# Second cross-attention: integer queries in 48 rows, with the scale applied during the search for the maximum

## The chip, the cores and the metric

The kernel runs on one core of one Trainium2 chip. The metric is the device time of one execution in microseconds (us). Three timed runs of the kernel before gave 736.27, 737.52 and 738.99 us, so the median is 737.52 us. One more execution was taken with the hardware profiler: its own time is 730.36 us, and all rows below come from it.

## The reference, cut to what matters

The program is two layers of a perceiver: cross-attention, a sequence mixer and a mixture of experts in each. The change touches the cross-attention of layer 1 alone. It has 256 query rows (x) and 4096 context rows, 16 heads of 16 channels:

```python
q = (x @ Wq + bq);  k, v = split(cond @ Wkv + bkv)      # 16 heads x 16 channels
q = _fq_sym(q * scale, axis=-1)    # s = max|q| / 127 over the 16 channels; round(q / s) * s
k = _fq_sym(k, axis=-1)            # the same for every key and head
v = _fq_sym(v, axis=2)
attn = softmax(einsum('bhqd,bhkd->bhqk', q, k))
attn = _fq_unsigned(attn, axis=-1) # round(attn / (max / 255)) * (max / 255)
out = einsum('bhqk,bhkd->bhqd', attn, v) @ Wp + bp
```

So each quantized query is an integer between -127 and 127 times one scale for each (query, head).

## The kernel before, in words

Two stages matter. Their queues are written out by hand: every engine has its own program, and semaphores order them. No scheduler moves anything.

**kv_stage** (names k_...) first makes the queries. TensorE multiplies the normed x with Wq (L1563), VectorE adds the bias (L1425), and quantize_queries (L1296 to L1321) quantizes them. The scores must be as exact as an f32 product, while TensorE is to run on bf16. So the quantized query (integer times scale, L1306) is split into three bf16 parts, and the quantized key likewise. Six products of parts are kept (PRODUCTS), which makes 6 x 16 = 96 rows of contraction for one head. The six columns of each query element are written by six casts: three copies of part 0 (L1315), a subtraction (L1318), two copies of part 1 (L1315), a subtraction (L1320), one copy of part 2 (L1321). All of this stands in VectorE's queue before the first step on the keys.

Then 16 steps of 256 keys each follow. In step m TensorE projects keys and values of step m+2 (L1575, L1577), VectorE quantizes the keys (L1446 to L1453), ScalarE and GpSimd split them into three bf16 parts (L1535, L1491, L1543, L1493), TensorE transposes the parts (L1592), and they are stored to kT_scratch in HBM (L1530). TensorE projects steps 0 and 1 in advance; the projection of step 2 waits until VectorE has read the keys of step 0 out of PSUM (semaphore k_read, from L1449). The transposes of step m wait for part 2 of the keys from GpSimd (L1493).

**xattn1_stage** (names d_...) handles the 16 heads one after the other. For one head there are 8 tiles ("quarters") j = 0..7: two halves of the queries (t) times four quarters (f) of 1024 keys. For each quarter:

- TensorE makes the scores, two matmuls of 512 columns (L1949), into one of three PSUM slots of 1024 columns (quarter). It waits for the ScalarE read that frees the slot.
- VectorE finds the negated maximum of each row over the 1024 columns (search, L1795). After four quarters L1799 combines four of them.
- ScalarE takes exp(score - maximum) with the sum (L1887).
- GpSimd scales and rounds the result to f16 (L1773). Half of the quarters are turned by DMA (L1736), the other half by TensorE (L1976), with copies out of PSUM by VectorE (L1807) and ScalarE (L1899). TensorE multiplies with the values (L1992) one head later. Once in a head VectorE rounds the values of that head (L1820).

The keys of a head come from kT_scratch in 6 DMAs of 16 rows (one for each product, L1723), issued on the SP queue. For heads 0 and 1 all 12 stand at the beginning; those of head m+2 stand behind the DMA transposes of head m. The stages run behind one another, with a barrier between them.

Of the kernel before, what the change touches and what calls it, by code (L numbers as in the profile page):

```python
# [22 lines left out]
NEG = 1e30  # L23
# [20 lines left out]
H, HD = 16, 16  # L44
# [1233 lines left out]
def layer1_memory(nc, d, g, sb, sem):  # L1278
    g["v"] = sb("v", [P, NKC, D])
    g["vam"] = sb("v_absmax", [P, D])  # L1280
    g["qs"] = sb("qs", [P, TC, H, 100], BF16)
    g["kT_stored"] = [sem(f"kT_stored{s}") for s in range(2)]
    g["w_inT"] = sb("w_inT", [P, KC, 2 * INNER])
    g["w_inT_in"] = sem("w_inT_in")
# [5 lines left out]
    g["w1_in"] = sem("w1_in")  # L1290


PRODUCTS = ((0, 0), (0, 1), (0, 2), (1, 0), (1, 1), (2, 0))
QROWS = len(PRODUCTS) * HD


def quantize_queries(nc, step, src, scaled, out, rest, s, rs, absmax, qs, done):

    f3, i3, q3, r3 = (a[:, :, :].rearrange("p t (h e) -> p (t h) e", e=HD) for a in (src, scaled, out, rest))
    axes = [P, TC * H, HD]  # L1300
    step(nc.vector.tensor_reduce(absmax, f3, AX.X, ALU.max, apply_absolute_value=True))
    step(nc.vector.tensor_scalar(s, absmax, 1.0 / 127.0, 1e-8, ALU.mult, ALU.max))
    step(nc.vector.reciprocal(rs, s))
    step(nc.vector.tensor_tensor(i3, f3, rs.unsqueeze(2).to_broadcast(axes), ALU.mult))
    step(nc.vector.tensor_scalar(i3, i3, ROUND, ROUND, ALU.add, ALU.subtract))
    step(nc.vector.tensor_tensor(q3, i3, s.unsqueeze(2).to_broadcast(axes), ALU.mult))  # L1306

    def columns(part):

        by_row = qs[:, :, :, 0:QROWS].rearrange("p t h (e j) -> p (t h) e j", j=len(PRODUCTS))  # L1310
        return [by_row[:, :, :, j] for j, (pq, _) in enumerate(PRODUCTS) if pq == part]

    def part_to(src_, part):
        for c in columns(part):
            step(nc.vector.tensor_copy(c, src_))  # L1315
        return columns(part)[0]
    p0 = part_to(q3, 0)
    step(nc.vector.tensor_tensor(r3, q3, p0, ALU.subtract))  # L1318
    p1 = part_to(r3, 1)
    step(nc.vector.tensor_tensor(q3, r3, p1, ALU.subtract))  # L1320
    nc.vector.tensor_copy(columns(2)[0], q3).then_inc(done, 1)  # L1321


def kv_stage(nc, d, g):
    ctx, sb, banks, sem = scope(nc)
# [3 lines left out]
    with ctx:  # L1329
# [10 lines left out]
        rest = [sb(f"k_rest{s}", [P, KPS, D]) for s in range(2)]  # L1340
        parts = [sb(f"k_parts{s}", [P, K_PARTS, KPS, D], BF16) for s in range(2)]
        kT = [sb(f"k_kT{s}", [P, K_PARTS * KC, KEYS], BF16) for s in range(2)]
        am = sb("k_absmax", [P, KPS * H])
        sc = sb("k_scale", [P, KPS * H])
# [52 lines left out]
        with nc.Block() as block:  # L1397
# [18 lines left out]
            def _(dve):  # L1416
# [7 lines left out]
                dve.wait_ge(q_psum, 1)  # L1424
                step(nc.vector.scalar_tensor_tensor(qf[:, :, :], ps[:, 5, :].rearrange("p (t c) -> p t c", t=TC), HD ** -0.5,  # L1425
                                                    bq[:, :].unsqueeze(1).to_broadcast([P, TC, D]), ALU.mult, ALU.add))
                quantize_queries(nc, step, qf, qi, qq, qr, sc[:, :], rs[:, :], am[:, :], g["qs"], qs_ready)
                lead = step.n

                def copy_turned(m, s, i):  # L1430
# [174 lines left out]
def xattn1_stage(nc, d, g):  # L1605
# [14 lines left out]
    with ctx:  # L1620
# [4 lines left out]
        qs = g["qs"]  # L1625
# [86 lines left out]
        with nc.Block() as block:  # L1712
# [66 lines left out]
            def _(dve):  # L1779
# [12 lines left out]
                def search(m, j):  # L1792
                    t, f = j // QT, j % QT
                    dve.wait_ge(scores_ready, m * APH + (j + 1))
                    nc.vector.tensor_reduce(nm[:, t, m:m + 1, f:f + 1], quarter(m, j).unsqueeze(1), AX.X, ALU.max,  # L1795
                                            negate=True).then_inc(nm_ready, 1)
                    if f == QT - 1:
                        dve.wait_ge(nm_ready, m * APH + (j + 1))
                        nc.vector.tensor_scalar(raised[:, :], nm[:, t, m, :], LOG255, NEG, ALU.add, ALU.min,  # L1799
                                                accum_out=mb[:, t, m, QT - 1:QT]).then_inc(mb_ready, 1)  # L1800
# [73 lines left out]
            def _(act):  # L1874
# [7 lines left out]
                def exps(m, j):  # L1882
                    t, f = j // QT, j % QT
                    act.wait_ge(nm_ready, m * APH + (j + 1))
                    if 1 <= m < H:
                        act.wait_ge(r_ready, m * APH + (j + 1 - APH))
                    nc.scalar.activation(e[j].unsqueeze(1), quarter(m, j).unsqueeze(1), ACT.Exp, bias=nm[:, t, m:m + 1, f],  # L1887
                                         accum_out=zp[:, t, m:m + 1, f]).then_inc(e_ready, 1)
                    if f == QT - 1:
                        act.wait_ge(mb_ready, m * TC + (t + 1))  # L1890
                        nc.scalar.activation(lift[t][:, :].unsqueeze(1), nm[:, t, m:m + 1, :], ACT.Exp, scale=-1.0,  # L1891
                                             bias=mb[:, t, m:m + 1, QT - 1]).then_inc(lift_ready, 1)
# [419 lines left out]
```

## Time and profile before

| | us |
|---|---|
| median of three timed runs | 737.52 |
| the profiled execution, its own time | 730.36 |
| its span | 728.7 |
| VectorE busy in the span | 494.4 (68%) |
| TensorE busy in the span | 624.3 (86%) |
| ScalarE busy in the span | 381.4 (52%) |
| GpSimd busy in the span | 334.5 (46%) |

The span is what the rows of the profile cover; the execution's own time is 1.7 us longer. The timed runs are about 7 us longer than the profiled one, so sums are made against the profiled one. The shares of busy time are averages over stages that have little in common: kv_stage runs from about 290 to 391 us, xattn1_stage from about 391 to 603 us, and each must be read by itself. A row of a list of instructions gives the start, the duration and, in brackets, how long the engine had been idle and what ended that. On VectorE an instruction may start while the last tens of nanoseconds of the one before it still show; the distance from start to start is what the queue pays.

### The profile page before, as it was taken

The page shows a single profiled execution, that of the slowest core. Times are in us where ns is not written, and L with a number is a line of the kernel's source. Part 1 is how long each engine was busy: PE and PEld are TensorE (multiplying, and loading weights), DVE is VectorE, ACT ScalarE, POOL GpSimd, SP SyncE. Part 2 cuts the span into 40 slices and gives each one's busy share as a digit, 9 for nine tenths or more (in the row PEclk, how much of TensorE's full clock was granted, in tenths as well). Part 3 has the DMA queues.
Part 4 walks back from the last instruction along what each step waited for, and adds up shares of the span by engine and source line. Part 5 has one row for each costly group of instructions (what it writes and reads, how often), then busy time and mean ns, then how long its engine had stood idle before and what let it go on. Part 6 is the DMA issues. An engine that isn't in the chain of part 4 may idle for free. (4 is left out here: it accounts for less than half of the span.)

```text
span 728.7 us, 13062 instructions
## 1 busy us (share of the span) xinstructions
PE 624.3 (86%) x4727; PEld 408.2 (56%) x4727; DVE 494.4 (68%) x813; ACT 381.4 (52%) x738; POOL 334.5 (46%) x261
## 2 busy tenths in 40 slices
PE   3767999986799999779995789888888889889997
PEld 1333445543577776558883155545554565667775
DVE  3268999974443333599994999999999955523222
ACT  1247865523211111336663899999999953222221
POOL 1039999981111110136651598898888940000000
PEclk9989999998699999979997596887879979999999
DMA  8827200004066660314444688788796938800000
GB/s 351 304 85 303 116 0 1 0 0 136 1 195 195 196 196 3 107 52 144 144 130 130 179 139 189 133 173 151 154 168 139 161 59 346 352 1 1 0 0 14
DMA packets 97030, 93.80 MB, mean 129 GB/s; under 512 B 70288, under 2 KB 87888, under 8 KB 92624
## 3 DMA queue, kind: packets, MB, share of 16 engines
q1 hardware_dynamic: 84432, 86.78, 43.5%
q10 hardware_dynamic: 12544, 6.29, 3.0%
q8 instruction: 34, 0.56, 0.3%
q14 instruction: 20, 0.16, 0.1%
HBM read 69.66 MB, written 6.62 MB: 105 GB/s over the span
## 5 line engine op out<-in xcount | busy, mean ns | idle before, releaser
L1795 DVE TENSOR_REDUCE d_nmax<-d_psum 128x1 f32<-128x1024 f32 x128 | 151.8, 1213 | 7.8 <-PE d_psum L1949 7.5
L1949 PE MATMUL d_psum<-d_kst,d_qT 96*128 96x512 bf16 x256 | 94.9, 465 | 27.6 <-DMA d_kst<-kT_scratch 10.6
L425 POOL TENSOR_TENSOR b_h<-b_h,b_cb 128x1024 f32<-128x1024 f32 x32 | 87.8, 2743 | 6.7 <-DVE b_h L475 5.1
L1887 ACT ACTIVATE d_e<-d_psum,d_nmax 128x1024 f32<-128x1024 f32 x64 | 71.4, 1120 | 14.8 <-DVE d_nmax L1795 14.1
L1773 POOL TENSOR_SCALAR d_rounded<-w_early,d_lift 128x1024 f16<-128x1024 f32 x62 | 70.1, 1131 | 14.0 <-ACT d_lift L1891 9.5
L1773 POOL TENSOR_SCALAR d_rounded<-d_e,d_lift 128x1024 f16<-128x1024 f32 x64 | 72.9, 1139 | 7.0 <-ACT d_lift L1891 1.3
L475 DVE TENSOR_TENSOR_SCAN b_h<-b_dA,b_psum 128x1024 f32<-128x1024 f32 x32 | 73.1, 2285 | 2.5 <-ACT b_dA L530 2.0
L1575 PE MATMUL k_psum<-k_wkv,k_ctxT 128*128 128x256 f32 x256 | 67.1, 394 | 6.2 <-issue 6.2
L1887 ACT ACTIVATE w_early<-d_psum,d_nmax 128x1024 f32<-128x1024 f32 x64 | 71.4, 1121 | 0.1
L530 ACT ACTIVATE b_dA<-b_dtT,b_A 128x248 f32<-128x248 f32 x128 | 53.7, 490 | 33.1 <-DVE b_h L475 28.1
L586 PE MATMUL b_psum<-b_bdiag,b_dtx 128*128 128x512 f32 x128 | 60.2, 594 | 0.8 <-DVE b_h L475 0.8
L1976 PEld LDWEIGHTS d_psum<-d_ident_f,d_rounded 128*128 128x128 f16 x512 | 41.8, 116 | 32.7 <-issue 21.7
L1575 PEld LDWEIGHTS k_psum<-k_wkv,k_ctxT 128*128 128x128 f32 x256 | 45.5, 198 | 16.9 <-issue 7.4
L1976 PE MATMUL d_psum<-d_ident_f,d_rounded 128*128 128x128 f16 x512 | 48.9, 252 | 6.8 <-ACT d_probsT L1899 3.6
L1949 PEld LDWEIGHTS d_psum<-d_kst,d_qT 96*128 96x128 bf16 x256 | 18.9, 108 | 57.7 <-ACT d_e L1887 26.4
L837 POOL TENSOR_TENSOR c_pick_weighed<-c_pick,c_w 128x384 f32<-128x384 bf16 x16 | 13.3, 833 | 81.2 <-PE c_psum L1033 74.3
L1992 PEld LDWEIGHTS d_psum<-d_vh,d_probsT 128*128 128x128 f16 x1024 | 42.9, 97 | 8.8 <-issue 4.0
L1992 PE MATMUL d_psum<-d_vh,d_probsT 128*128 128x16 f16 x1024 | 43.5, 170 | 2.3 <-issue 1.6
L607 PE MATMUL b_psum<-b_h,ident 128*128 128x256 f32 x128 | 36.1, 404 | 6.9 <-DVE b_h L482 4.4
L872 DVE TENSOR_TENSOR c_a<-c_silu,c_psum 128x192 f32<-128x192 f32 x16 | 5.7, 354 | 52.9 <-ACT c_silu L932 52.9
L607 PEld LDWEIGHTS b_psum<-b_h,ident 128*128 128x128 f32 x128 | 21.8, 189 | 33.9 <-DVE b_h L482 32.2
L1232 PE MATMUL f_psum<-w,f_xnT 128*128 (+1 forms) x128 | 40.5, 459 | 0.0
(396 smaller groups left out, 1194.1 us busy)
## 6 DMA issues: line engine op xcount, KB each, us to landing
d_kst<-kT_scratch SPq DMA_DIRECT2D x96, 128.0 KB, 2.8
w<-in_w SPq DMA_DIRECT2D x8, 1088.0 KB, 20.3
b_cb<-c_scratch SPq DMA_DIRECT2D x4, 2048.0 KB, 6.8
w_early<-in_w0gu SPq DMA_DIRECT2D x8, 768.0 KB, 5.2
w_late<-in_w0gu SPq DMA_DIRECT2D x8, 768.0 KB, 5.1
kT_scratch<-k_kT ACTq DMA_DIRECT2D x16, 384.0 KB, 2.8
a_ctxT<-in_ctxT SPq DMA_DIRECT2D x2, 2048.0 KB, 12.2
a_ctx<-in_ctx SPq DMA_DIRECT2D x2, 2048.0 KB, 20.6
```

Source lines behind the costliest of these rows:

```text
L425: nc.gpsimd.tensor_tensor(hv, hv, cv, ALU.mult).then_inc(hc_ready, 1)
L475: nc.vector.tensor_tensor_scan(h[s][:, :], dA[s % 2][:, :], ps[:, 2 * (s % 2):2 * (s % 2) + 2, :] .rearrange("p a b -> p (a b)"), 0.0, ALU ...
L530: nc.scalar.activation(out[:, :, j, :, 1:L], src, ACT.Exp, scale=A[:, c, n * NT + j:n * NT + j + 1]).then_inc(dA_ready, 1)
L586: last = nc.tensor.matmul(ps[:, 2 * (s % 2) + t, :], dtx[:, t, c * P:(c + 1) * P], bdiag[t][:, n * NT:n * NT + NT, :], start=True, stop=True)
L607: last = nc.tensor.matmul(ps[:, 4 + c, 0:T], ident[:, :], hv[:, j], start=False, stop=False, skip_group_check=True)
L1575: nc.tensor.matmul(psum_kv(s, part)[:, j, :], cT[s][:, k, j * P:(j + 1) * P], wkv[:, k, cols], start=(k == 0), stop=False)
L1773: nc.gpsimd.tensor_scalar(tile_of(r, j), e[j], lift[t][:, f:f + 1], HALF_ULP_ONE, ALU.mult, ALU.add).then_inc(r_ready, 1)
L1795: nc.vector.tensor_reduce(nm[:, t, m:m + 1, f:f + 1], quarter(m, j).unsqueeze(1), AX.X, ALU.max, negate=True).then_inc(nm_ready, 1)
L1887: nc.scalar.activation(e[j].unsqueeze(1), quarter(m, j).unsqueeze(1), ACT.Exp, bias=nm[:, t, m:m + 1, f], accum_out=zp[:, t, m:m + 1, f]). ...
L1949: last = nc.tensor.matmul(quarter(m, j)[:, b * 512:(b + 1) * 512], qT[0:QROWS, m:m + 1, t * P:(t + 1) * P], kst[m % 2][0:QROWS, at:at + 51 ...
L1976: last = nc.tensor.transpose(turn_tile(m, j)[:, b * P:(b + 1) * P], tile_of(r, j)[:, b * P:(b + 1) * P], ident16[:, :])
L1992: last = nc.tensor.matmul(out, pT[m % 2][:, t, b, :], vh[m % 2][:, b, :], start=(b == 0), stop=(b == NKC - 1 and t not in BY_DMA))
```

## The change

The query is kept as its integer, which is exact in one bf16 part, so only three products are left (integer with each of the three key parts), and a head has 48 rows in place of 96. The scale is not in the product any more. The negated scale of each query and head goes into a new tile, minus_sq. The search does three things in one instruction: it multiplies the 1024 scores in PSUM by the negated scale, writes them back to the same place, and takes the minimum of the results (accum_out). ScalarE's exp reads the negated scores with scale=-1.0.

```diff
-PRODUCTS = ((0, 0), (0, 1), (0, 2), (1, 0), (1, 1), (2, 0))
+PRODUCTS = ((0, 0), (0, 1), (0, 2))
...
-    g["qs"] = sb("qs", [P, TC, H, 100], BF16)
+    g["qs"] = sb("qs", [P, TC, H, 52], BF16)
+    g["minus_sq"] = sb("minus_q_scale", [P, TC, H])
...
     step(nc.vector.tensor_scalar(i3, i3, ROUND, ROUND, ALU.add, ALU.subtract))
-    step(nc.vector.tensor_tensor(q3, i3, s.unsqueeze(2).to_broadcast(axes), ALU.mult))
...
-    p0 = part_to(q3, 0)
-    step(nc.vector.tensor_tensor(r3, q3, p0, ALU.subtract))
-    p1 = part_to(r3, 1)
-    step(nc.vector.tensor_tensor(q3, r3, p1, ALU.subtract))
-    nc.vector.tensor_copy(columns(2)[0], q3).then_inc(done, 1)
+    step(nc.vector.tensor_scalar(minus_s.rearrange("p t h -> p (t h)"), s, -1.0, None, ALU.mult))
+    by_row = qs[:, :, :, 0:QROWS].rearrange("p t h (e j) -> p (t h) e j", j=len(PRODUCTS))
+    nc.vector.tensor_copy(by_row, i3.unsqueeze(3).to_broadcast(axes + [len(PRODUCTS)])).then_inc(done, 1)
...
                 def search(m, j):
-                    nc.vector.tensor_reduce(nm[:, t, m:m + 1, f:f + 1], quarter(m, j).unsqueeze(1), AX.X, ALU.max,
-                                            negate=True).then_inc(nm_ready, 1)
+                    nc.vector.tensor_scalar(quarter(m, j), quarter(m, j), g["minus_sq"][:, t, m:m + 1], NEG, ALU.mult, ALU.min,
+                                            accum_out=nm[:, t, m, f:f + 1]).then_inc(nm_ready, 1)
...
-                    nc.scalar.activation(e[j].unsqueeze(1), quarter(m, j).unsqueeze(1), ACT.Exp, bias=nm[:, t, m:m + 1, f],
+                    nc.scalar.activation(e[j].unsqueeze(1), quarter(m, j).unsqueeze(1), ACT.Exp, scale=-1.0, bias=nm[:, t, m:m + 1, f],
```

The lines of the changed kernel are numbered 14 lower from kv_stage on, and in quantize_queries they are shifted as well. Its order of instructions stands beside that of before at three places. VectorE's queue in kv_stage, from the rounding of the query (k_qi) to the first step on the keys; before:

```order
L1305 TENSOR_SCALAR k_qi<-k_qi 128x512
L1306 TENSOR_TENSOR k_qq<-k_qi,k_scale 128x512
L1315 CAST qs<-k_qq 128x32x16 x3
L1318 TENSOR_TENSOR k_qrest<-k_qq,qs 128x512
L1315 CAST qs<-k_qrest 128x32x16 x2
L1320 TENSOR_TENSOR k_qq<-k_qrest,qs 128x512
L1321 CAST qs<-k_qq 128x32x16
L1446 TENSOR_REDUCE k_absmax<-k_psum 128x32
```

and now:

```order
L1306 TENSOR_SCALAR k_qi<-k_qi 128x512
L1307 TENSOR_SCALAR minus_q_scale<-k_scale 128x32
L1309 CAST qs<-k_qi 128x32x48
L1432 TENSOR_REDUCE k_absmax<-k_psum 128x32
L1433 TENSOR_SCALAR k_scale<-k_absmax 128x32
```

Nine instructions of 512 elements are gone; one of 32 elements and one of 1536 elements stand in their place. VectorE's queue in xattn1_stage, one head from the rounding of its values (d_vh) on; before:

```order
L1820 TENSOR_SCALAR d_vh<-d_vh_scaled 128x512
L1795 TENSOR_REDUCE d_nmax<-d_psum 128x1 x3
L1812 COPY d_o<-d_psum 128x2x16
L1795 TENSOR_REDUCE d_nmax<-d_psum 128x1
L1799 TENSOR_SCALAR d_nmax_raised,d_mm_log<-d_nmax 128x4
L1795 TENSOR_REDUCE d_nmax<-d_psum 128x1
L1807 TENSOR_SCALAR d_probsT<-d_psum 128x1024
```

and now:

```order
L1806 TENSOR_SCALAR d_vh<-d_vh_scaled 128x512
L1781 TENSOR_SCALAR d_psum,d_nmax<-d_psum,minus_q_scale 128x1024 x3
L1798 COPY d_o<-d_psum 128x2x16
L1781 TENSOR_SCALAR d_psum,d_nmax<-d_psum,minus_q_scale 128x1024
L1785 TENSOR_SCALAR d_nmax_raised,d_mm_log<-d_nmax 128x4
L1781 TENSOR_SCALAR d_psum,d_nmax<-d_psum,minus_q_scale 128x1024
L1793 TENSOR_SCALAR d_probsT<-d_psum 128x1024
```

Nothing moves there; each search is another kind of instruction with two outputs and one more input. The SP queue from the start of xattn1_stage, with the loads of the keys (d_kst); before:

```order
L1723 DMA d_kst<-kT_scratch 16x4096 x12
L1728 DMA d_wp<-in_wp 128x512
L1728 DMA d_bp<-in_bp 128x256
L1729 DMA w_inT<-in_w_inT 128x2048
L1736 DMA_TRANSPOSE d_probsT<-d_rounded 128x16x128 x2
L1723 DMA d_kst<-kT_scratch 16x4096 x6
```

and now:

```order
L1709 DMA d_kst<-kT_scratch 16x4096 x6
L1714 DMA d_wp<-in_wp 128x512
L1714 DMA d_bp<-in_bp 128x256
L1715 DMA w_inT<-in_w_inT 128x2048
L1722 DMA_TRANSPOSE d_probsT<-d_rounded 128x16x128 x2
L1709 DMA d_kst<-kT_scratch 16x4096 x3
```

Half of the loads are gone, and the rest keep their place behind the transposes.

## Rows read from the trace of the kernel before

**Rows 1.** Busy time by engine in four stretches: three of kv_stage, one of xattn1_stage.

```profile
core 0: us, PE busy (x) PEld busy (x) DVE busy (x) ACT busy (x) POOL busy (x), PEclk, DMA share, GB/s
308.20:314.40 6.20, 0.03 (x1) 0.00 (x0) 5.93 (x10) 0.00 (x0) 0.00 (x0) 0.68 0.15 42
314.40:320.00 5.60, 5.57 (x14) 4.04 (x15) 5.36 (x10) 1.75 (x3) 2.49 (x2) 0.50 0.00 0
...
325.00:382.00 57.00, 57.00 (x394) 46.86 (x393) 53.55 (x98) 38.95 (x49) 34.51 (x26) 1.00 0.48 139
...
412.20:586.90 174.70, 149.02 (x2110) 93.29 (x2110) 170.86 (x242) 168.68 (x300) 154.15 (x136) 0.84 0.83 155
```

**Rows 2.** Who waited for whom from 412.2 to 586.9 us: total, times, longest.

```profile
PE d_psum L1949 <- DMA d_kst<-kT_scratch: 5.8, 7, 1.2
...
DVE d_nmax L1795 <- PE d_psum L1949: 2.4, 9, 0.4
```

**Rows 3.** VectorE in order of time, one head: start us, us, instruction.

```profile
481.87 0.43 DVE L1820 TENSOR_SCALAR d_vh<-d_vh_scaled 128x512 f16<-128x512 f32 x1
482.22 3.48 DVE L1795 TENSOR_REDUCE d_nmax<-d_psum 128x1 f32<-128x1024 f32 x3
...
486.96 0.16 DVE L1799 TENSOR_SCALAR_CACHE_REDUCE d_nmax_raised<-d_nmax 128x4 f32<-128x4 f32 x1
487.04 0.08 DVE L1799 DVE_READ_ACCUMULATOR d_nmax_raised<-d_nmax 128x1 f32 x1
487.04 1.22 DVE L1795 TENSOR_REDUCE d_nmax<-d_psum 128x1 f32<-128x1024 f32 x1
...
492.96 0.85 DVE L1820 TENSOR_SCALAR d_vh<-d_vh_scaled 128x512 f16<-128x512 f32 x1
```

**Rows 4.** VectorE's groups by form: busy us, mean ns of one, idle before.

```profile
L1795 DVE TENSOR_REDUCE d_nmax<-d_psum 128x1 f32<-128x1024 f32 x128 | 151.8, 1213 | 7.8 <-PE d_psum L1949 7.5
L475 DVE TENSOR_TENSOR_SCAN b_h<-b_dA,b_psum 128x1024 f32<-128x1024 f32 x32 | 73.1, 2285 | 2.5 <-ACT b_dA L530 2.0 <-PE b_psum L586 0.4
...
L1446 DVE TENSOR_REDUCE k_absmax<-k_psum 128x32 f32<-128x512 f32 x16 | 11.0, 688 | 1.1
...
L454 DVE TENSOR_SCALAR b_h<-b_psum,b_cols 128x256 f32<-128x256 f32 x2 | 1.0, 485 | 0.1
...
L448 DVE TENSOR_SCALAR b_psum<-b_psum 128x512 f32<-128x512 f32 x1 | 0.7, 700 | 1.1 <-ACT b_psum L509 1.1
...
L443 DVE COPY b_drT<-b_psum 128x256 f32<-128x256 f32 x1 | 0.4, 425 | 2.1 <-PE b_psum L552 2.1
```

**Rows 5.** VectorE in order of time, the query's quantization.

```profile
301.98 0.18 DVE L1302 TENSOR_SCALAR k_scale<-k_absmax 128x32 f32<-128x32 f32 x1
...
303.77 0.69 DVE L1306 TENSOR_TENSOR k_qq<-k_qi,k_scale 128x512 f32<-128x512 f32 x1
304.50 3.18 DVE L1315 CAST qs<-k_qq 128x512 bf16<-128x512 f32 x3
...
312.36 0.64 DVE L1446 TENSOR_REDUCE k_absmax<-k_psum 128x32 f32<-128x512 f32 x1
```

**Rows 6.** TensorE, then GpSimd, in order of time, the first steps on the keys.

```profile
314.44 2.04 PE L1575 MATMUL k_psum<-k_wkv,k_ctxT 128*128 128x256 f32 x4 [6.20 <-issue]
...
320.33 1.19 PE L1575 MATMUL k_psum<-k_wkv,k_ctxT 128*128 128x256 f32 x4
...
323.17 1.03 PE L1575 MATMUL k_psum<-k_wkv,k_ctxT 128*128 128x256 f32 x4
...
324.15 1.03 PE L1575 MATMUL k_psum<-k_wkv,k_ctxT 128*128 128x256 f32 x4
```

```profile
318.34 1.16 POOL L1493 TENSOR_TENSOR k_parts<-k_rest,k_parts 128x512 bf16<-128x512 f32 x1 [0.74 <-ACT k_parts L1543]
```

**Rows 7.** All engines in order of time, the start of xattn1_stage.

```profile
393.75 7.55 SPq L1723 DMA_DIRECT2D d_kst<-kT_scratch  x12
...
399.59 2.72 PE L1949 MATMUL d_psum<-d_kst,d_qT 96*128 96x512 bf16 x6 [4.80 <-DMA d_kst<-kT_scratch]
```

More of the change, by code:

```diff
@@ L1290, in layer1_experts, with quantize_queries @@
     g["w1_in"] = sem("w1_in")
-PRODUCTS = ((0, 0), (0, 1), (0, 2), (1, 0), (1, 1), (2, 0))
+PRODUCTS = ((0, 0), (0, 1), (0, 2))
 QROWS = len(PRODUCTS) * HD
-def quantize_queries(nc, step, src, scaled, out, rest, s, rs, absmax, qs, done):
-    f3, i3, q3, r3 = (a[:, :, :].rearrange("p t (h e) -> p (t h) e", e=HD) for a in (src, scaled, out, rest))
+def quantize_queries(nc, step, src, scaled, s, rs, absmax, qs, minus_s, done):
+    f3, i3 = (a[:, :, :].rearrange("p t (h e) -> p (t h) e", e=HD) for a in (src, scaled))
     axes = [P, TC * H, HD]
@@ L1305, in quantize_queries @@
     step(nc.vector.tensor_scalar(i3, i3, ROUND, ROUND, ALU.add, ALU.subtract))
-    step(nc.vector.tensor_tensor(q3, i3, s.unsqueeze(2).to_broadcast(axes), ALU.mult))
[L1308 to L1316, printed above, removed]
-    p0 = part_to(q3, 0)
-    step(nc.vector.tensor_tensor(r3, q3, p0, ALU.subtract))
-    p1 = part_to(r3, 1)
-    step(nc.vector.tensor_tensor(q3, r3, p1, ALU.subtract))
-    nc.vector.tensor_copy(columns(2)[0], q3).then_inc(done, 1)
+    step(nc.vector.tensor_scalar(minus_s.rearrange("p t h -> p (t h)"), s, -1.0, None, ALU.mult))
+    by_row = qs[:, :, :, 0:QROWS].rearrange("p t h (e j) -> p (t h) e j", j=len(PRODUCTS))
+    nc.vector.tensor_copy(by_row, i3.unsqueeze(3).to_broadcast(axes + [len(PRODUCTS)])).then_inc(done, 1)
 def kv_stage(nc, d, g):
@@ L1351, in kv_stage @@
         qi = sb("k_qi", [P, TC, D])
-        qq = sb("k_qq", [P, TC, D])
-        qr = sb("k_qrest", [P, TC, D])
         ps = banks("k_psum")
@@ L1426, in _ @@
                                                     bq[:, :].unsqueeze(1).to_broadcast([P, TC, D]), ALU.mult, ALU.add))
-                quantize_queries(nc, step, qf, qi, qq, qr, sc[:, :], rs[:, :], am[:, :], g["qs"], qs_ready)
+                quantize_queries(nc, step, qf, qi, sc[:, :], rs[:, :], am[:, :], g["qs"], g["minus_sq"][:, :, :], qs_ready)
                 lead = step.n
```

## The prediction

> **What bounds the kernel now.** I read the busy time by stretches first, then the waits inside the two stages that the change touches, then VectorE in order of time, and last the groups by form, for prices.
>
> From 412.2 to 586.9 us, which is 15 heads of the second cross-attention, VectorE is busy 170.86 of 174.70 us and ScalarE 168.68 [rows 1]. VectorE waits there only 2.4 us in nine short waits, all for scores [rows 2]. So its queue sets the pace: 174.7 / 15 = 11.65 us for one head. The shortest head is 11.09 us, from 481.87 to 492.96 [rows 3]. Three searches take 3.48 us in a row there, with the last one shown at its full 1.21, so searches start 1.13 us apart: 1.21 less an overlap of 0.08. Eight of them are 9.1 us of the 11.09. The mean head is 0.56 longer: 0.16 is the waits (2.4 / 15), and much of the rest is the rounding of the values, which took 0.43 us in one head and 0.85 in the next [rows 3].
>
> In kv_stage TensorE is busy 57.00 of 57.00 us once the steps on the keys run [rows 1]: it sets the pace there. But before that it stands idle for 6.20 us, from 308.2 to 314.44, until VectorE has got through the queries and has read the keys of step 0. The granted clock is then at its lower level (0.50, or 1.2 GHz) from 314.4 to 320 [rows 1, 6].
>
> **Part 1: the query's quantization.** From L1306 to the first L1446 VectorE spends 312.36 - 303.77 = 8.59 us [rows 5]. All of it goes. What comes instead is a negation of 32 elements, 0.18 us as the same form L1302 and 0.04 to the next start, and one copy that writes 1536 elements. No row shows that form. Below, one strided cast of today, 3.18 / 3 = 1.06 us [rows 5], if its 512 reads are what costs. Above, three of them, 3.18 us, if each written element costs. Its destination is contiguous, not stepped as today's, so I take one element a clock: 1.13 us for 1024 [rows 3] makes 1.7 for 1536. VectorE reaches the keys 8.59 - 0.22 - 1.7 = 6.7 us earlier (5.2 to 7.3).
>
> TensorE then starts the projection of step 2 at once, at 308.2, and saves 6.2 us of idle time. It also never drops its clock: three groups took 320.33 - 314.44 = 5.89 us at the lower clock, against 0.98 each later (324.15 - 323.17) [rows 6], so 2.95 more. Something new is late next. The transposes of step 0 stand in TensorE's queue behind that projection and need part 2 from GpSimd, which ended at 318.34 + 1.16 = 319.50 [rows 6] and now ends 6.7 earlier, at 312.8, while the projection ends at 308.2 + 3.9 = 312.1. That is a wait of 0.7 us; I allow the step after it the same again, and a little more, 1.6 in all. While TensorE waits, the projection and the transposes behind it wait too. Gain: 6.2 + 2.95 - 1.6 = 7.5 us (6.0 to 8.5). As TensorE bounds the rest of the stage, nothing there gives it back.
>
> **Part 2: the loads of the keys.** Twelve DMAs take 7.55 us to issue, 0.63 each, and TensorE waits for head 0's six, until 399.59 [rows 7]. With three in place of six it starts 3 x 0.63 = 1.9 us earlier (1.0 to 2.0). Later heads have three DMAs less each. TensorE waited 5.8 us for those keys in seven heads [rows 2], but it is up to three quarters ahead, and little of that reached VectorE: of its 2.4 us of waits I credit 1.6 to earlier keys and to a VectorE that asks later. Half as many rows leave the length of a matmul alone (it streams 512 columns either way), so TensorE's work on scores costs the same: 0.
>
> **Part 3: the search, 128 times.** Three things are new in it.
> - Its kind and its write to PSUM. A reduction over 512 elements of PSUM takes 688 ns, a tensor_scalar from PSUM back to the same PSUM 700 ns [rows 4]: 0 to +12 ns. It works at one element a clock both ways. I take 3.
> - The scale, one value for each partition. With one such operand 256 elements from PSUM take 485 ns, a copy without one 425 [rows 4]: +60 ns. [...]
> - The minimum, read out by a second instruction. In L1799 that reading shows 83 ns, but it starts 0.08 after the main part and the next search starts in the same hundredth: 487.04 and 487.04 [rows 3]. The price in the queue is 0, and it ends with the main part. That is behind 4 elements; behind 1024 it could be the whole 0.08. I take 0, because it is the only row of this pair.
>
> So 128 x 0.064 = +8.2 us on VectorE's queue (0 to 18.4). Nothing else queued there is shorter, so it all stands on the path, apart from the 1.6 us above: +6.6. ScalarE works 168.68 / 15 = 11.2 us a head, below VectorE's new 11.09 + 0.51 = 11.6. exp with a constant scale is the instruction of before: 0.
>
> The reading of the accumulator is where the Trainium skill disagrees. The page "VectorE: DVE Perf Modes", section "Two Vector instructions with no wait between them", says that an operation with an accumulator output is two instructions, and "Vector Engine (DVE) Microarchitecture Reference", section 5.2, gives about 75 ns of fixed cost to each instruction after overlap. By that the readings would add 128 x 0.075 = 9.6 us. The trace agrees on two instructions, but not on their price: 0.00 from start to start [rows 3]. The same section names no price for a scalar operand, and by it alone the search would be as long as now; the row of L454 against L443 says 60 ns.
>
> **The sum.** -7.5 - 1.9 + 6.6 = -2.8 us. Against the profiled execution's 730.36 us that is 727.6. The timed runs were 7.2 us above it; the same difference on their median gives 737.52 - 2.8 = 734.7 us. Its own range, from the bounds of parts 1 and 2 and a rounding of the values that may fall into step with GpSimd by some 0.2 us a head either way (3 us): 731 to 738.5.
>
> **Rivals.**
> 1. The reading costs its 0.08 us behind a long stream. Place: between any two searches, 128 times. 128 x 0.08 = +10.2, net +7.4: 745. It decides against the change as soon as a reading costs more than 0.02 us (2.8 / 128). For it: the instruction is 83 ns long; against it: 32 pairs in which the next one doesn't wait.
> 2. The search doesn't get longer: scale and reading vanish in the overlap, or the new kind has a shorter fixed part. Part 3 is then 0, and of the 1.6 us of waits only what earlier keys take away stays, a quarter of it, 0.4: -7.5 - 1.9 - 0.4 = -9.8, 727.7. Against it is L454.
> 3. Multiplying and accumulating together take two clocks an element, as the scan does: 2285 ns for 1024 [rows 4]. 128 x 1.07 = +137, about 865. For it: also a chain of multiply and combine; against it: the reduction keeps one a clock with an accumulator of its own.
> 4. Part 1 isn't passed on: TensorE, freed early, waits for the split of the keys on ScalarE and GpSimd in every step. 7.5 becomes 0: +4.7, 742.2. For it: TensorE and GpSimd are nearly level (57.00 against the chain that it waits for); against it: GpSimd is busy only 34.51 of 57.00 [rows 1].
>
> **How the numbers follow.** A measurement of this kernel can tell about 0.5%, 3.7 us, from no change. My forecast gets 0.51, rival 1 0.19, rival 2 0.17, rival 3 0.06, rival 4 0.05, and 0.02 is for what I haven't seen. Faster by over 0.5% (below 733.8): rival 2 and four tenths of the forecast, 0.37. Slower by over 0.5% (above 741.2): rivals 1, 3 and most of 4, 0.31. The rest, 0.32, is within. The range takes in the forecast, rival 1 and nearly all of rival 2, and leaves out rival 3: 727 to 746. The likeliest case alone is 731 to 738.5.
>
> **What would show it.** In the changed profile: the search as a main part of about 1.27 us and a reading of 0.08, with searches in a row 1.19 us apart (1.27 for rival 1, 1.13 for rival 2, over 2.2 for rival 3); a head of about 11.6 us at the shortest; the copy of the query at about 1.7 us; no idle time of TensorE over 1.5 us between its projections of steps 1 and 2, and a granted clock of 1.00 there; the stage of the keys 7 to 8 us shorter; the first scores about 4 us after SP starts to issue keys, not 5.8. The prediction is wrong if VectorE isn't busy over 95% of the heads any more, if searches are further apart than 1.22 us, or if TensorE waits in every step on the keys.

## The result and the profile after

The changed kernel takes 766.88 us (median of 4 runs, 765.86 to 770.47), the kernel before 738.25 in runs beside it: a ratio of 1.040 (1.035 to 1.044), so 28.6 us slower. Forecast were 734.7 and a range of 727 to 746. The profiled execution of after took 765.86 us, with a span of 764.0, against 728.7 before: 35.3 us more. The execution profiled before was itself 7.9 us under the median given here, so the two traces lie further apart than the medians. The kernel before took 727 to 747 us over the sessions, so each experiment is judged by its ratio to runs of that kernel taken beside it, fast runs against fast ones; by the means of all runs, x1 and x5 below would both be 1.007 in place of 1.009 and 1.014, and no other ratio moves by over 0.003.

By stage, from the two traces: the work ahead of the queries (not changed) takes 2.1 us less. The stage of the keys, from k_qf (the bias added to the queries) to the first load of keys, takes 93.5 us, 93.2 before. From that load to the first scores it is 6.0, 5.8 before, and from the first scores to the end of the attention 238.7, 201.7 before. So all of the loss is in the heads, and nothing was gained ahead of them.

**The heads.** Busy time by engine of after in four stretches of heads, to be held against the last row of [rows 1]:

```profile
core 0: us, PE busy (x) PEld busy (x) DVE busy (x) ACT busy (x) POOL busy (x), PEclk, DMA share, GB/s
...
440.00:480.00 40.00, 40.00 (x400) 20.22 (x396) 34.53 (x67) 32.84 (x57) 30.32 (x27) 0.50 0.61 101
480.00:520.00 40.00, 40.00 (x422) 20.48 (x420) 34.50 (x70) 33.15 (x57) 28.61 (x26) 0.50 0.55 103
520.00:560.00 40.00, 40.00 (x421) 20.27 (x420) 34.58 (x70) 32.79 (x58) 28.41 (x26) 0.50 0.64 110
560.00:600.00 40.00, 40.00 (x420) 20.16 (x418) 34.51 (x67) 33.53 (x57) 29.13 (x27) 0.50 0.56 110
```

TensorE is busy without a gap in these stretches, and its granted clock is 0.50 (1.2 GHz) throughout; before it was 0.84 on average, with TensorE busy 149.0 of 174.7 us [rows 1]. VectorE, which set the pace before at 98%, is at 86%. Every head but the first takes 14.13 us, against a mean of 11.64 before: 15 heads are 14.03 on average, so 15 x 2.39 = 35.8 of the stage's 37.0 us.

The groups by form over the 15 heads of after, and what VectorE waits for in the same stretch (us in total, times, longest):

```profile
L1781 DVE TENSOR_SCALAR_CACHE_REDUCE d_psum<-d_psum,minus_q_scale 128x1024 f32<-128x1024 f32 x120 | 153.4, 1290 | 25.3 <-PE d_psum L1935 22.8
L1935 PE MATMUL d_psum<-d_kst,d_qT 48*128 48x512 bf16 x238 | 117.8, 621 | 1.3 <-ACT d_e L1873 1.0 <-ACT w_early L1873 0.3
```

```profile
DVE d_psum L1781 <- PE d_psum L1935: 22.8, 29, 1.1
```

So VectorE now waits 22.8 us for scores, against 2.4 before [rows 2]. The score matmul, the same 512 columns, takes 621 ns; before, from the same kind of view:

```profile
L1949 PE MATMUL d_psum<-d_kst,d_qT 96*128 96x512 bf16 x238 | 86.0, 453 | 19.2 <-ACT d_e L1887 6.8 <-DMA d_kst<-kT_scratch 5.8 <-ACT w_early L1887 5.5
```

The search itself, VectorE of after in order of time, against [rows 3]:

```profile
480.67 1.29 DVE L1781 TENSOR_SCALAR_CACHE_REDUCE d_psum<-d_psum,minus_q_scale 128x1024 f32<-128x1024 f32 x1
481.88 0.14 DVE L1781 DVE_READ_ACCUMULATOR d_psum<-d_psum,minus_q_scale 128x1 f32 x1
481.88 1.29 DVE L1781 TENSOR_SCALAR_CACHE_REDUCE d_psum<-d_psum,minus_q_scale 128x1024 f32<-128x1024 f32 x1
```

1.29 us long, 1.21 from start to start; 1.13 before. The reading starts with the next search in the same hundredth.

**The stage of the keys.** VectorE of after in order of time, the end of the query's work (against [rows 5]):

```profile
301.20 0.43 DVE L1306 TENSOR_SCALAR k_qi<-k_qi 128x512 f32<-128x512 f32 x1
301.66 0.18 DVE L1307 TENSOR_SCALAR minus_q_scale<-k_scale 128x32 f32<-128x32 f32 x1
301.88 0.96 DVE L1309 CAST qs<-k_qi 128x1536 bf16<-128x1536 f32 x1
302.76 0.68 DVE L1432 TENSOR_REDUCE k_absmax<-k_psum 128x32 f32<-128x512 f32 x1
```

The 8.59 us are 302.76 - 301.66 = 1.10 now: VectorE comes 7.5 us earlier. TensorE doesn't stand idle at the start any more, and its clock stays at 1.00:

```profile
302.00:307.90 5.90, 5.90 (x32) 4.70 (x31) 5.66 (x11) 1.71 (x3) 1.20 (x1) 1.00 0.20 56
```

Yet the stage isn't shorter, because each step got longer. GpSimd and VectorE around one instruction, k_ki, before and then after:

```profile
337.72 0.43 DVE L1451 TENSOR_SCALAR k_ki<-k_ki 128x512 f32<-128x512 f32 x1
...
338.39 1.51 POOL L1493 TENSOR_TENSOR k_parts<-k_rest,k_parts 128x512 bf16<-128x512 f32 x1 [1.85 <-ACT k_parts L1543]
...
342.37 0.43 DVE L1451 TENSOR_SCALAR k_ki<-k_ki 128x512 f32<-128x512 f32 x1
```

```profile
340.27 1.15 POOL L1479 TENSOR_TENSOR k_parts<-k_rest,k_parts 128x512 bf16<-128x512 f32 x1 [1.00 <-ACT k_parts L1529]
...
340.45 1.25 DVE L1437 TENSOR_SCALAR k_ki<-k_ki 128x512 f32<-128x512 f32 x1
...
341.48 0.84 PE L1578 MATMUL k_psum<-ident_bf,k_parts 128*128 128x128 bf16 x12 [0.34 <-POOL k_parts L1479]
...
345.69 1.26 DVE L1437 TENSOR_SCALAR k_ki<-k_ki 128x512 f32<-128x512 f32 x1
```

Before, k_ki starts 0.7 us ahead of GpSimd's second subtraction and takes 0.43; steps are 4.65 us apart. After, it starts 0.18 behind that subtraction, ends 0.28 behind its end and takes 1.25; steps are 5.25 apart, and TensorE waits for GpSimd in each of them (0.3 to 0.4 us, and 1.8 at the end of the loop). The Trainium skill ("SBUF — State Buffer", section "Who interferes with whom") has the rule: VectorE and GpSimd share a port pair under an exclusive lock, tensor_scalar can need both ports, and whoever starts first holds the pair to the end. The trace agrees: once the steps are 5.25 us apart, k_ki ends just behind GpSimd's instruction and never inside it. Before, GpSimd's second subtraction was the longer one, 1.44 to 1.61 us against 1.15 now, and the steps were shorter all the same.

**The first scores.** TensorE's wait there, of after (against [rows 7]):

```profile
396.35 1.15 POOL L1736 PARTITION_ALL_REDUCE d_v_absmax<-v_absmax  x1 [12.95 <-issue]
...
397.38 0.28 POOL L1737 MEMSET d_minus<- 128x128 f16 x1
...
397.92 2.71 PE L1935 MATMUL d_psum<-d_kst,d_qT 48*128 48x512 bf16 x6 [4.21 <-POOL d_minus L1737]
```

The keys need three loads instead of six, but TensorE waits for a GpSimd memset that stands behind an all-reduce.

### The profile page after: what moved, and what is told of

Its sections match the earlier page's. It is cut to its first block and busy times, and to the rows that moved or that the text cites. A ratio compares the mean times of both kernels' runs of the same rounds, so it can differ in the third digit from the quotient of the medians.

```text
span 764.0 us, 13135 instructions
## 1 busy us (share of the span) xinstructions
PE 683.8 (89%) x4727; PEld 418.4 (55%) x4727; DVE 509.8 (67%) x934; ACT 385.6 (50%) x738; POOL 328.8 (43%) x261
## 5 line engine op out<-in xcount | busy, mean ns | idle before, releaser
L1781 DVE TENSOR_SCALAR_CACHE_REDUCE d_psum<-d_psum,minus_q_scale 128x1024 f32<-128x1024 f32 x128 | 163.3, 1289 | 29.9 <-PE d_psum L1935 27.3
L1935 PE MATMUL d_psum<-d_kst,d_qT 48*128 48x512 bf16 x256 | 126.7, 621 | 9.7 <-ACT d_e L1873 4.4
L1873 ACT ACTIVATE d_e<-d_psum,d_nmax 128x1024 f32<-128x1024 f32 x64 | 71.3, 1114 | 36.6 <-DVE d_psum L1781 35.8
L1962 PEld LDWEIGHTS d_psum<-d_ident_f,d_rounded 128*128 128x128 f16 x512 | 49.5, 142 | 52.9 <-POOL d_rounded L1759 39.0
L1962 PE MATMUL d_psum<-d_ident_f,d_rounded 128*128 128x128 f16 x512 | 66.1, 311 | 2.1 <-POOL d_rounded L1759 1.8
L1561 PE MATMUL k_psum<-k_wkv,k_ctxT 128*128 128x256 f32 x256 | 64.0, 381 | 0.0
L1561 PEld LDWEIGHTS k_psum<-k_wkv,k_ctxT 128*128 128x128 f32 x256 | 43.7, 190 | 9.9
L1935 PEld LDWEIGHTS d_psum<-d_kst,d_qT 48*128 48x128 bf16 x256 | 21.4, 116 | 47.8 <-issue 33.9
L1978 PE MATMUL d_psum<-d_vh,d_probsT 128*128 128x16 f16 x1024 | 45.8, 175 | 0.0
```

Source lines behind the costliest of these rows:

```text
L1561: nc.tensor.matmul(psum_kv(s, part)[:, j, :], cT[s][:, k, j * P:(j + 1) * P], wkv[:, k, cols], start=(k == 0), stop=False)
L1781: nc.vector.tensor_scalar(quarter(m, j), quarter(m, j), g["minus_sq"][:, t, m:m + 1], NEG, ALU.mult, ALU.min, accum_out=nm[:, t, m, f:f + ...
L1935: last = nc.tensor.matmul(quarter(m, j)[:, b * 512:(b + 1) * 512], qT[0:QROWS, m:m + 1, t * P:(t + 1) * P], kst[m % 2][0:QROWS, at:at + 51 ...
L1962: last = nc.tensor.transpose(turn_tile(m, j)[:, b * P:(b + 1) * P], tile_of(r, j)[:, b * P:(b + 1) * P], ident16[:, :])
L1978: last = nc.tensor.matmul(out, pT[m % 2][:, t, b, :], vh[m % 2][:, b, :], start=(b == 0), stop=(b == NKC - 1 and t not in BY_DMA))
```

## The experiments

Theory for the heads: the number of rows of the score matmul (its contraction) decides which clock is granted. 48 rows hold it at 0.50, TensorE becomes the bound, and the search costs what was forecast. Rivals: the new search, the number of loads, or the values in the rows do it. Theory for the keys: the steps are long because of the order in which GpSimd and VectorE meet, and a single delay decides it.

### Rows of the score matmul

**x1: the change with each product twice (96 rows).**

```diff
-PRODUCTS = ((0, 0), (0, 1), (0, 2))
+PRODUCTS = ((0, 0), (0, 1), (0, 2)) * 2
...
-    step(nc.vector.tensor_scalar(minus_s.rearrange("p t h -> p (t h)"), s, -1.0, None, ALU.mult))
+    step(nc.vector.tensor_scalar(minus_s.rearrange("p t h -> p (t h)"), s, -0.5, None, ALU.mult))
```

> The changed kernel with 96 rows again: the three products stand twice and the scale is halved, so the search, the queries and the result are those of the change, and only the contraction's rows (48 to 96) and the key loads (3 to 6 a head) go back. Theory (the rows decide the granted clock): the clock in the heads returns to about 0.84 as before, TensorE leaves the bound, and a head takes 12.1 us (11.65 of before and 0.06 for each of 8 searches) in place of 14.13: about 32 us less than the changed kernel, 733 to 745. Rival (the slower search holds the clock down, or its writes to PSUM do): the clock stays 0.50 and the time 765 or more.

739.26 us, ratio 1.0089 (1.0045 to 1.0132); heads 12.27 us on average, the granted clock of a head 0.59 to 1.00. Doubling the rows takes back three quarters of the loss. It brings back the six loads a head as well; x5 below keeps three.

**x2: the kernel before with 48 rows and its plain search** (only the first part of the query is kept; less is computed).

```diff
-PRODUCTS = ((0, 0), (0, 1), (0, 2), (1, 0), (1, 1), (2, 0))
+PRODUCTS = ((0, 0), (0, 1), (0, 2))
-    p0 = part_to(q3, 0)
...
+    for c in columns(0)[:-1]:
+        step(nc.vector.tensor_copy(c, q3))
+    nc.vector.tensor_copy(columns(0)[-1], q3).then_inc(done, 1)
```

> The kernel before with 48 rows alone: the queries keep only their first bf16 part, which leaves out the parts that carry the rest of their precision; the search is the plain reduction of before. Theory of the rows: the clock is 0.50 in all heads, a head takes 14.1 us as in the changed kernel, and the whole is near 766 (kv_stage a little different). Rival of the search: the clock stays near 0.84 and the time is near 735.

770.79 us, ratio 1.048 (1.040 to 1.056), heads at 14.13 us. Without the new search the whole loss is there. Its windows, then those of x1:

```profile
480.00:520.00 40.00, 40.00 (x412) 20.53 (x413) 32.68 (x47) 33.54 (x58) 28.39 (x26) 0.50 0.54 106
```

```profile
480.00:520.00 40.00, 35.28 (x467) 22.65 (x467) 39.76 (x81) 37.82 (x66) 34.01 (x30) 0.74 0.80 147
```

x2 has VectorE at 32.7 of 40 us and the clock at 0.50, x1 has VectorE back at 39.8.

**x4: 96 rows whose second 48 have zero queries** (the keys under them are real).

```diff
-PRODUCTS = ((0, 0), (0, 1), (0, 2))
+PRODUCTS = ((0, 0), (0, 1), (0, 2)) * 2
...
-    nc.vector.tensor_copy(by_row, i3.unsqueeze(3).to_broadcast(axes + [len(PRODUCTS)])).then_inc(done, 1)
+    nc.vector.tensor_copy(by_row[:, :, :, 0:3], i3.unsqueeze(3).to_broadcast(axes + [3])).then_inc(done, 1)
...
+                step(nc.vector.memset(g["qs"][:, :, :, :].rearrange("p t h c -> p (t h c)"), 0.0))
```

> As the 96-row version of the changed kernel, but the extra 48 rows hold zeros in the queries (keys are loaded there), with the scale unhalved. If what counts is how many rows an instruction names, the clock is again about 0.84 and the time that of the doubled version. If it counts what is really multiplied (data), the clock stays at 0.50 and the time near 766.

743.3 us, ratio 1.0096 (1.0052 to 1.0139), heads 12.26 us. The rows count whether their query values are zero or not.

**x5, z2, z1: the changed kernel with its 48 rows padded by zeros to 128, 80 and 64.** Three key loads a head as in the change; VectorE zeroes the buffers once, at the start of the attention stage; the first loads and TensorE wait for that (these waits are left out below).

```diff
+MROWS = 128   # z2: 80, z1: 64
...
-kst = [sb(f"d_kst{s}", [QROWS, NK], BF16) for s in range(2)]
+kst = [sb(f"d_kst{s}", [MROWS, NK], BF16) for s in range(2)]
...
+for a in (kst[0][:, :], kst[1][:, :], qT[:, :, :]):
+    nc.vector.memset(a, 0.0).then_inc(zeroed, 1)
...
-... matmul(..., qT[0:QROWS, ...], kst[m % 2][0:QROWS, at:at + 512])
+... matmul(..., qT[0:MROWS, ...], kst[m % 2][0:MROWS, at:at + 512])
```

> The changed kernel with its 48 rows padded by zeros to 128: the two key buffers and the turned queries are zeroed once by VectorE, the three key DMAs and everything else are as in the change. The first DMAs wait for that zeroing, so the first scores come a few us later than in the changed kernel. Theory (the number of rows in the score matmuls holds the granted clock down): heads of 11.8 to 12.3 us in place of 14.13, a granted clock over 0.70 in the heads, TensorE no longer busy without a gap, about 736 to 744 us. Rival (zeros don't count, or it is the number of DMAs, or the new search): heads of 14.1 us at 0.50, 766 to 772 us.

> The changed kernel with its 48 rows padded by zeros to 80. By the same readings: between the two levels a mean head of 12.4 to 13.3 us; on the 48-row side 14.13 us; on the 96-row side 12.3 us and about 745 us.

> The changed kernel with its 48 rows padded by zeros to 64 (as x5, with 64 in place of 128). If the granted clock follows the number of rows step by step, a level between 48 rows (heads of 14.13 us, clock 0.50) and 96 rows (12.27 us, 0.6 to 1.0): some heads at 0.50, a mean head of 13 to 13.8 us. If 64 rows are still on the 48-row side, 14.13 us in every head and about 772 us (the changed kernel's 767 and some 5 for the zeroing at the start); if on the other side, 12.3 us and about 745.

x5: 743.02 us, ratio 1.0141 (1.0047 to 1.0234; four runs, so the interval is wide), heads 12.24; the zeroing makes the first scores 3.6 us later, which is in its time. z2 (one run): 742.68 us, heads 12.25. z1 (one run): 774.13 us, heads 14.13. The same stretch of the three, 128, 80 and 64 rows:

```profile
480.00:520.00 40.00, 31.72 (x479) 19.48 (x476) 39.62 (x82) 37.68 (x67) 34.08 (x31) 0.93 0.75 128
```

```profile
480.00:520.00 40.00, 35.69 (x452) 23.33 (x453) 39.74 (x82) 37.89 (x68) 34.03 (x31) 0.76 0.76 124
```

```profile
480.00:520.00 40.00, 40.00 (x398) 20.31 (x397) 35.46 (x69) 33.99 (x59) 28.41 (x26) 0.50 0.56 102
```

With the work unchanged otherwise, 64 rows are on the 48-row side, and 80 on the 96-row side: it turns between, in one jump of the head's length and not step by step as z1's and z2's first reading would have it. 128 rows raise the clock further (0.93), but the heads are hardly shorter, because VectorE bounds them.

**x6: the kernel before, its 96 rows padded to 128** (the same edit, but only the 32 added rows are zeroed, and the loads don't wait for it).

> The kernel before with its 96 rows padded by zeros to 128. Theory (more rows, higher granted clock): the heads that ran at about 0.70 in the kernel before rise toward 1.00; heads of 11.1 to 11.3 us on average in place of 11.64, which is 3 to 8 us less: 728 to 733 us. Rival (96 rows are already past the point at which rows matter): within 1 us of the kernel before, 736 us, heads as before.

736.33 us, ratio 1.0005 (0.9949 to 1.0062), heads 11.68: a miss. The rival's numbers came, and 728 to 733 us didn't. The clock did rise, to 0.90 over the 15 heads against 0.84 [rows 1], but VectorE bounds these heads too: it is busy 170.84 of their 175.24 us.

**x3: the changed kernel with 16 dummy matmuls ahead of the scores of heads 2, 6 and 10.**

```diff
+if j == 0 and m in (2, 6, 10):
+    keep_warm(nc, g, quarter(m, j)[:, 0:512], 16)
```

> The changed kernel with 16 extra matmuls of 128 rows by 512 columns ahead of the scores of heads 2, 6 and 10. If the low clock is only a matter of never having been raised, the first push (7 us at the low clock) raises it and it stays: heads of 12.1 us afterwards and 745 us in all. If the stream of 48-row scores cannot hold it, the clock goes back to 0.50 within a few us of each push, heads are 14.1 us again, and the whole is 766 plus about 15.

780.04 us (one run). The pushed heads show 0.70 to 0.71 and are 16.6 to 17.0 us long; all heads between them are back at 0.50 and 14.13. A push lifts the clock within its own head only, so the low clock isn't a state that was merely entered badly.

### The search

**y2: the kernel before with the new search alone**, by a column of -1.

```diff
-nc.vector.tensor_reduce(nm[...], quarter(m, j)..., ALU.max, negate=True)
+nc.vector.tensor_scalar(quarter(m, j), quarter(m, j), g["minus_one"][:, :], NEG, ALU.mult, ALU.min, accum_out=nm[...])
...
+nc.scalar.activation(..., ACT.Exp, scale=-1.0, ...)
```

> The kernel before with the new search alone: the multiplication is by a column of -1, the exponential has scale -1, everything else (queries, 96 rows, loads) as before. Theory (the search costs 1.21 us from start to start in place of 1.13, and its dependents start 0.14 later): heads 0.6 to 0.8 us longer on average, 12.2 to 12.4 us against 11.64 in the profile, 9 to 12 us in all: a ratio of 1.012 to 1.017. By the record's own forecast of 0.064 us each it would be 6.6 us, 1.009. The stage of the keys stays as before, steps of 4.65 us.

743.18 us, ratio 1.0098 (1.0056 to 1.014): 7.2 us. That is between the two sizes named and under the range of my theory (1.012 to 1.017). Heads 12.26 us. Its search group, with VectorE's waits for scores at the end of the row:

```profile
L1797 DVE TENSOR_SCALAR_CACHE_REDUCE d_psum<-d_psum,minus_one 128x1024 f32<-128x1024 f32 x120 | 151.1, 1284 | 0.7 <-PE d_psum L1951 0.7
```

### The stage of the keys

**x7: the changed kernel with eight more copies of the queries**, which makes VectorE as late for the keys as before.

```diff
+for _ in range(8):
+    step(nc.vector.tensor_copy(by_row, i3.unsqueeze(3).to_broadcast(axes + [len(PRODUCTS)])))
```

> The changed kernel with the copy of the queries made nine times in place of once, which gives VectorE about 7 us back ahead of the keys (8 x 0.88). Theory (part 1's gain is given back because VectorE's wide tensor_scalar k_ki falls under GpSimd's work once VectorE comes early): TensorE stands idle for about 6 us before step 0's transposes and runs cold for some us, but k_ki goes back to about 460 ns and the steps to 4.65 us, so the stage of the keys is as long as in the changed kernel, 93 to 94 us. Rival (something else in the change makes the steps 5.25 us): k_ki stays at about 1190 ns, steps at 5.25, the stage 100 us. The heads stay at 14.13 us either way.

778.83 us (one run). My theory missed, the rival's numbers came: TensorE idled 6.5 us, and k_ki still took 1.25 us and a step 5.25. So VectorE's lateness isn't what kept the steps of before short. What differed from the kernel before was TensorE's clock behind the idle time. Before, it was low for three groups, until 320.33 [rows 6], and the transposes of step 0 came 2.7 us behind the start of step 1's k_ki (321.47 - 318.78). In x7 the clock was back after some 3 us, and they came 1.05 behind. ScalarE's copy of the turned keys, and GpSimd behind it, then came 0.8 us earlier: just ahead of the next k_ki. Before, then x7:

```profile
318.78 0.99 DVE L1451 TENSOR_SCALAR k_ki<-k_ki 128x512 f32<-128x512 f32 x1
...
321.47 0.83 PE L1592 MATMUL k_psum<-ident_bf,k_parts 128*128 128x128 bf16 x12
```

```profile
322.58 1.00 DVE L1439 TENSOR_SCALAR k_ki<-k_ki 128x512 f32<-128x512 f32 x1
...
323.63 0.83 PE L1580 MATMUL k_psum<-ident_bf,k_parts 128*128 128x128 bf16 x12
```

That the clock behind the idle time chose the order is read from these two traces; no run changes the clock there alone. From this the theory of a single delay, which the next run tests.

**y1: the changed kernel with one instruction more on ScalarE, in step 0's copy alone.**

```diff
+if isinstance(m, int) and m == 0:
+    nc.scalar.activation(kT[s][:, 0:3, :], psT[s][:, 0:3, :], ACT.Copy).then_inc(k_kick, 1)
+    act.wait_ge(k_kick, 1)
 nc.scalar.activation(kT[s][:, :, :], psT[s], ACT.Copy).then_inc(kT_ready, 1)
```

> The changed kernel with one instruction more in the whole stage of the keys: ScalarE copies half of step 0's turned keys once more ahead of the full copy, which makes everything behind it on ScalarE about 0.8 us later, once. Theory (two orders lock in: where GpSimd's second subtraction starts just ahead of VectorE's k_ki, VectorE's 0.43 us instruction is held to 1.25 and a step takes 5.25 us; where it starts behind k_ki, 0.43 and 4.65): from the step after the delay on k_ki takes 0.43 us, steps are 4.65 us apart, and the stage from k_qf to the first key DMA of the next takes about 85 us in place of 93.5. Rival (the steps are long because of what the change made of the stage's buffers and instructions): the one delay moves one step, k_ki stays at 1.25 and the stage takes 93.5 to 94.5 us. Heads stay at 14.13 us.

757.26 us (one run), the stage 86.0 us in place of 93.5. All engines in order of time: the added copy, GpSimd and VectorE right behind it and two steps on:

```profile
313.47 0.80 ACT L1514 ACTIVATE k_kT<-k_psum 128x768 bf16<-128x768 bf16 x1
...
315.69 0.43 DVE L1438 TENSOR_SCALAR k_ki<-k_ki 128x512 f32<-128x512 f32 x1
...
316.35 1.50 POOL L1480 TENSOR_TENSOR k_parts<-k_rest,k_parts 128x512 bf16<-128x512 f32 x1 [1.85 <-ACT k_parts L1533]
...
320.34 0.43 DVE L1438 TENSOR_SCALAR k_ki<-k_ki 128x512 f32<-128x512 f32 x1
...
325.00 0.43 DVE L1438 TENSOR_SCALAR k_ki<-k_ki 128x512 f32<-128x512 f32 x1
```

0.8 us more work, once, makes each later step 0.6 us shorter than in the changed kernel. 93.2 - 86.0 = 7.2 us is the gain that part 1 was forecast to bring (7.5).

**y4 and z3: the kernel before (96 rows, plain search) with its query casts merged by part, with the one delay and without.**

```diff
-for c in columns(part): step(nc.vector.tensor_copy(c, src_))
+step(nc.vector.tensor_copy(by_row[:, :, :, at[0]:at[-1] + 1], src_.unsqueeze(3).to_broadcast(axes + [len(at)])))
```

> The kernel before with plain search and 96 rows, its query casts merged by part (three casts of part 0 become one broadcast copy, two of part 1 one) and the one delay of ScalarE. VectorE reaches the keys 2.2 us + 1.0 us = about 3.2 us earlier, TensorE idles 3 us in place of 6.2; steps stay at 4.65 us, because the order behind k_ki is kept. Theory: 3 to 6 us faster than the kernel before, ratio 0.992 to 0.996. Rival (TensorE's clock recovers as late as before, and what VectorE saves is lost in the first steps): within 1 us.

> y4 without the one delay of ScalarE: the kernel before with only its query casts merged. In y4 the clock was back at 317.0, and the transposes of step 0 started 2.5 us behind the start of step 1's k_ki, against 2.7 in the kernel before and 1.05 in the locked order of x7. Theory: without the delay GpSimd's second subtraction still starts some 0.4 us behind k_ki, so steps stay at 4.65 us, and the 0.3 us that the delay cost in one step comes back: 3 us off the stage, ratio 0.986 to 0.995, level with y4. Rival (the delay was what kept the order): k_ki goes to 1.25 us, steps to 5.25, ratio 1.00 to 1.01.

y4: 728.28 us, ratio 0.9894 (0.9844 to 0.9945): faster than both kernels. z3: 737.32 us, ratio 1.001 (0.9974 to 1.0047). I had z3 wrong: an earlier VectorE falls into the long steps by itself. z3, then y4:

```profile
318.63 1.16 POOL L1494 TENSOR_TENSOR k_parts<-k_rest,k_parts 128x512 bf16<-128x512 f32 x1 [1.00 <-ACT k_parts L1544]
...
318.81 1.26 DVE L1452 TENSOR_SCALAR k_ki<-k_ki 128x512 f32<-128x512 f32 x1
```

```profile
320.46 0.43 DVE L1453 TENSOR_SCALAR k_ki<-k_ki 128x512 f32<-128x512 f32 x1
...
321.77 1.16 POOL L1495 TENSOR_TENSOR k_parts<-k_rest,k_parts 128x512 bf16<-128x512 f32 x1 [2.50 <-ACT k_parts L1548]
```

Their stages take 98.1 and 90.4 us: 7.7 us between them, and 1.16% of the time between the ratios, which is 8.5 us. All runs with the added copy on ScalarE (y1, y3, y4) have the short steps, and of the runs without it only those that quantize the queries as the kernel before does (before, x6, y2). Of y4's 7.8 us against the kernel before the stage explains 2.8; its heads (11.79 us) were no shorter than in the trace of before. The interval reaches down to 4 us; what the rest is stays open.

**y3: 96 rows as x1, the delay, and the memset of x8.**

> The changed kernel with its three products twice (96 rows, as in x1), the one delay of ScalarE and GpSimd's memset ahead of its partition_all_reduce. Theory: x1's 1.0089 times the kernel before (+6.6 us) less 8 to 8.5 us in the stage of the keys, and up to 1 us at the first scores where six keys' DMAs may take its place: 733 to 735 us where the kernel before takes 736 (ratio 0.995 to 0.999). Rival (no second order): as x1, 1.009.

733.6 us, ratio 0.9978 (0.9939 to 1.0017): 1.1% below x1, as expected, and not to be told from the kernel before.

**x8: the changed kernel with GpSimd's memset ahead of its all-reduce.**

```diff
+nc.gpsimd.memset(unlift[:, :], -HALF_ULP_ONE).then_inc(ident_ready, 1)
 nc.gpsimd.partition_all_reduce(vall[:, :], g["vam"][:, :], P, RMAX).then_inc(vall_ready, 1)
-nc.gpsimd.memset(unlift[:, :], -HALF_ULP_ONE).then_inc(ident_ready, 1)
```

> The changed kernel with GpSimd's memset ahead of its partition_all_reduce at the start of the attention stage. Theory (TensorE waits for that memset and no longer for keys): first score 4.0 to 4.6 us after SP issues the first key DMA, against 6.0 in the changed kernel, and a TensorE wait for keys in place of the wait for GpSimd; 1.4 to 2 us off the stage. Rival (the keys themselves land only at about that time): first score stays 5.7 to 6.0 us behind. The heads stay at 14.13 us.

767.45 us (one run). TensorE starts 5.0 us behind the first load and waits for keys:

```profile
398.05 2.23 PE L1935 MATMUL d_psum<-d_kst,d_qT 48*128 48x512 bf16 x6 [3.61 <-DMA d_kst<-kT_scratch]
```

1.0 us gained at this place (the whole time of one run doesn't show it), not the 1.4 to 2 expected: the memset held TensorE back, but three loads bring the first scores forward by 0.8 us and not by 1.9.

## Why the prediction was wrong

- **The step that failed: "Half as many rows leave the length of a matmul alone (it streams 512 columns either way), so TensorE's work on scores costs the same: 0."** At one clock it holds: six score matmuls took 2.72 us with 96 rows [rows 7] and 2.71 with 48, both at 0.50. But the granted clock went down with the rows, and one score matmul of the heads went from 453 to 621 ns on average. The step cost 15 heads x (14.03 - 12.27) = 26 us, by after against x1. None of the rivals had TensorE becoming the bound in the heads, though TensorE was busy 85% of them at a mean clock of 0.84 [rows 1]. It had little room, and the text never priced it at the lower clock. Of the three signs of being wrong that it named, two came (VectorE busy 86% of the heads, TensorE waiting in every step on the keys); the third, searches over 1.22 us apart, didn't.
- **Part 1, 7.5 us: right in itself, and given back.** VectorE came 7.5 us earlier (6.7 forecast, the copy 0.88 us from start to start instead of 1.7), TensorE lost neither the idle time nor the clock. What failed is "As TensorE bounds the rest of the stage, nothing there gives it back". The steps went from 4.65 to 5.25 us apart, which over 13 steps is 7.8 us. y1 shows the 7.2 us once they don't. Rival 4 had the result (part 1 gives 0) and gave TensorE's wait in every step as its sign, with a chance of 0.05. It lacked the cause, VectorE held up by GpSimd (k_ki 1.25 us for 0.43); 34.51 of 57.00 us of GpSimd's busy time was the wrong evidence, since it is not how much it works but when it starts.
- **Part 2: 1.9 us forecast, nothing came.** The memset behind the all-reduce had been hidden behind six loads. Without it 1.0 us came (x8).
- **Part 3: +6.6 us forecast, 7.2 measured (y2).** The scalar's 60 ns, 3 for the new kind and a reading without a price made 0.063 (the text reckons with 0.064); the spacing went up by 0.08, and no run prices the three apart. In the traces the 15 heads of y2 are 9.3 us longer than those of before; the ratio's interval, 4.1 to 10.3 us, holds that too. The reading of the accumulator starts with the next search, so rival 1's mechanism isn't there. The remaining 0.02 I can't assign, and with an interval that wide it says little that 6.6 and 7.2 lie close. The dependents of a search start 0.14 us later (L1785 1.39 us behind the search's start, 1.25 before).
- With rows kept at 96 the change would have ended at +6.6 us (x1): still slower, inside the range forecast. The loss beyond is the clock. (A slip beside it: the chances of rivals 1, 3 and 4 add up to 0.30, so most of them can't be 0.31.)

## What to carry to other kernels

A smaller contraction wasn't free on TensorE here, though each matmul streams the same columns. Look at the granted clock before and after, price TensorE's work at the lower level, and if it would then be the bound, try padding the rows (zeros did as well as data here). In a loop over several engines look at which of VectorE and GpSimd starts first where one of them takes longer than alone: here an order stayed for the whole loop, and work taken off ahead of the loop tipped it the wrong way. A delay of 0.8 us, once, was then worth 7.5 us of the stage (y1) and 7.7 (y4 against z3).

## What the runs showed of the hardware

- 48 or 64 rows in the score matmuls: a granted clock of 0.50 with TensorE busy 40.00 of 40.00 us. 80, 96 and 128 rows: 0.74 to 0.93 in the same stretch and, but for the rows, the same search and queries, with TensorE less busy (z2, x1, x5). 80 and 64 rows have one run each. The Trainium skill ("TensorE: Matmul & The Clock Gate", section "What's actually happening") ties the clock to how busy TensorE has been; here a TensorE busy without a gap stays at the lower level. Why the rows decide the clock, these runs don't show.
- Extra rows with zero values raise the clock like others (x4, x5).
- Two stable orders of one and the same loop, 4.65 and 5.25 us a step, with k_ki 0.43 or 1.25 us long; in each of the 17 traces the order, once there, stayed to the end of the loop.
- An accumulator reading of 0.14 us behind 1024 elements starts with the next instruction: 0.00 from start to start.
- A cast that writes 1536 bf16 from 512 f32 read three times takes 0.96 us; each of the three strided casts of 512 took 1.06 [rows 5].
